# Differential attention in a four-layer kernel: the order of TensorE's products, and where a head's factor is multiplied in

## The reference

```python
L1 = einsum(l2norm(q1), l2norm(k1)) * cos_scale        # b, h, n, m; h = 8 heads, 8 channels each
L2 = einsum(l2norm(q2), l2norm(k2)) * cos_scale
G  = tanh(delta_gain[h] * (L1 - L2))
A1 = softmax(L1 + G)
A2 = softmax(L2 - G)
y  = einsum(A1 - lambda_full * A2, v)
y  = y * rsqrt(mean(y * y) + eps) * subln_weight * 0.5
out = y @ Wo.T + bo
```

## Time and profile before

| | |
|---|---|
| median of 3 runs | 797.56 us (795.8 to 797.76) |
| profiled execution | 796.23 us, span of its instructions 794.0 us |
| busy: TensorE, VectorE, ScalarE, GpSimd | 660.3, 564.8, 485.4, 228.4 us |
| chain of waits that ended last | TensorE 50%, VectorE 30%, ScalarE 11% |
| mean granted TensorE clock | 0.976 of 2.4 GHz |

### The profile page before, as it was taken

The page is one execution under the profiler, slowest core; times in us unless marked ns, Lnnn a source line. Parts: engine busy times, 40 slices in busy tenths (PEclk is TensorE's granted clock), DMA queues, the critical chain, the costliest instruction groups (busy, mean ns, idle before and its releaser), DMA issues.

```text
span 794.0 us, 9725 instructions
## 1 busy us (share of the span) xinstructions
PE 660.3 (83%) x3476; PEld 282.5 (36%) x3514; DVE 564.8 (71%) x1087; ACT 485.4 (61%) x468; POOL 228.4 (29%) x359
## 2 busy tenths in 40 slices
PE   4999899999999478887878788778787787979796
PEld 2576545454544112222221122122222111456364
DVE  5656321407161688888999889999988999768756
ACT  1344323233334359999999999889899989422311
POOL 3601100101014475312434513743933002011001
PEclk9999999999999679999999999999999999999998
DMA  8000200000000110011100111010110013300250
GB/s 296 1 1 1 82 1 0 1 0 1 0 1 0 27 27 14 14 28 28 27 14 19 23 27 28 15 25 15 28 27 14 14 27 107 107 1 14 62 165 27
DMA packets 16752, 26.00 MB, mean 33 GB/s; under 512 B 2496, under 2 KB 7360, under 8 KB 16320
## 3 DMA queue, kind: packets, MB, share of 16 engines
q1 hardware_dynamic: 16704, 25.38, 11.6%
HBM read 15.87 MB, written 1.11 MB: 21 GB/s over the span
## 4 chain that ended last, share of the span: by engine, by line
PE 50%; DVE 30%; ACT 11%; issue 7%; DMA 1%; POOL 0%; SPq 0%; POOLq 0%; ACTq 0%; DVEq 0%
DVE hid L1115 10%; DVE hid L1112 9%; PE ps L512 7%; PE ps L522 7%; ACT probs L821 7%; PE ps L600 6%; PE ps L593 5%; PE ps L612 4%; PE ps L499 3%; ACT w_hh L851 3%; PE ps L621 3%; PE ps L532 2%; PE ps L419 2%; PE ps L450 2%; PE ps L545 2%
## 5 line engine op out<-in xcount | busy, mean ns | idle before, releaser
L851 ACT ACTIVATE w_hh<-hid 128x2048 f32<-128x2048 f32 x128 | 243.8, 1905 | 12.0 <-DVE hid L1115 12.0
L593 PE MATMUL ps<-q_s,k_s 128*128 128x512 bf16 (+1 forms) x474 | 163.4, 394 | 32.4 <-DVE hid L1112 22.2
L1112 DVE TENSOR_TENSOR hid<-ps,probs 128x1024 f32<-128x1024 f32 x128 | 156.3, 1221 | 37.2 <-ACT probs L821 35.9
L821 ACT ACTIVATE probs<-ps,gain 128x1024 f32<-128x1024 f32 x128 | 142.2, 1111 | 40.2 <-PE ps L593 37.0
L1115 DVE SCALAR_TENSOR_TENSOR hid<-ps,probs 128x1024 f32<-128x1024 f32 x128 | 155.4, 1214 | 0.0
L600 PE MATMUL ps<-w_hh,v_h 128*32 128x512 f32 x1024 | 139.4, 617 | 5.4 <-issue 4.4
L593 PE MATMUL ps<-q_w,k_w 64*128 64x512 bf16 x256 | 97.8, 396 | 54.6 <-DVE hid L1115 53.0
L593 PEld LDWEIGHTS ps<-q_s,k_s 128*128 128x128 bf16 (+1 forms) x512 | 42.0, 96 | 148.0 <-DVE hid L1112 60.4
L1449 POOL TENSOR_SCALAR rs<-mv 128x4 f32<-128x4 f32 x32 | 7.4, 231 | 256.5 <-DVE mv L930 256.4
L1023 DVE SCALAR_TENSOR_TENSOR hid<-ps,s_b,rot 128x512 f32<-128x512 f32 x16 | 11.9, 750 | 87.1 <-ACT rot L794 87.1
L877 ACT ACTIVATE u_q<-ps 128x512 f32<-128x512 f32 x32 | 19.1, 598 | 67.8 <-PE ps L612 67.7
(11 more groups left out here) (249 smaller groups left out, 923.3 us busy)
## 6 DMA issues: line engine op xcount, KB each, us to landing
k_w<-k_s SPq DMA_DIRECT2D x32, 128.0 KB, 2.3
q_w<-q_s SPq DMA_DIRECT2D x32, 128.0 KB, 2.3
w_hh<-w_rows SPq DMA_DIRECT2D x4, 1024.0 KB, 10.6
w_hh<-in_b_h SPq DMA_DIRECT2D x2, 1024.0 KB, 8.6
hid<-w_rows SPq DMA_DIRECT2D x2, 1024.0 KB, 6.2
part<-w_rows SPq DMA_DIRECT2D x8, 256.0 KB, 7.3
x_res<-in_x SPq DMA_DIRECT2D x4, 256.0 KB, 6.1
tab<-in_rope SPq DMA_DIRECT2D x1, 1024.0 KB, 7.0
```

The lines of the kernel that those rows point to most:

```text
L593: last = mm(ps[:, base + half, :], k_op[rows, u, keys], q_op[rows, u, half * CHUNK:(half + 1) * CHUNK], start=True, stop=True)
L821: A(gg[:, mt % 2, :], banks[:, 0:2 * CHUNK], ACT.Tanh, scale=gain[:, u:u + 1]).then_inc(S["g"], 1)
L851: A(ee[:, mt % 2, :], zz[:, mt % 2, :], ACT.Exp).then_inc(S["e"], 1)
L1112: v.tensor_tensor(zz[:, mt % 2, 0:SEQ], banks[:, 2 * CHUNK:4 * CHUNK], gg[:, mt % 2, :], ALU.add).then_inc(S["z1"], 1)
```

## The change

The scale of the logits is multiplied by the head's gain before it goes into the queries, so that TensorE's products are gain times L1 and gain times L2, and tanh needs no scale. The two sums multiply the products by the inverse of the gain and by its negative, read through a pointer; the first becomes a scalar_tensor_tensor. The gain is kept between 1e-20 and 1e20 in magnitude. The gain copies on GpSimd and their semaphore go. On TensorE a step's order becomes: difference product (s+2), turn, first component (s+2), values (s), second component (s+2).

```diff
@@ c_table
+            gain = sm[:, SM_GAIN:SM_GAIN + HEADS]
+            me.step(v.scalar_tensor_tensor(tiny[:, 24:32], gain, -1.0, gain, ALU.mult, ALU.max))
+            me.mark(v.tensor_scalar(tiny[:, 24:32], tiny[:, 24:32], GAIN_LOW, GAIN_HIGH, ALU.max, ALU.min))
+            me.step(v.tensor_scalar(tiny[:, 32:40], gain, 0.0, None, ALU.is_ge))
+            me.step(v.tensor_scalar(tiny[:, 32:40], tiny[:, 32:40], 2.0, -1.0, ALU.mult, ALU.add))
+            me.step(v.tensor_tensor(tiny[:, 24:32], tiny[:, 24:32], tiny[:, 32:40], ALU.mult))
+            me.mark(v.tensor_tensor(tiny[:, 8:16], tiny[:, 8:16], tiny[:, 24:32], ALU.mult))
+            me.step(v.reciprocal(gain_inv[:, 0], tiny[:, 24:32]))
+            me.mark(v.tensor_scalar(gain_inv[:, 1], gain_inv[:, 0], -1.0, None, ALU.mult))
@@ TensorE
-            c_scores(0, 0, 0)
-            c_scores(1, 0, 1)
+            for mt in range(2):
+                c_diff(mt, 0, mt)
+                c_first(mt, 0, mt)
+                c_second(mt, 0, mt)
             for n in range(NH):
                 for mt in range(BT):
                     s = n * BT + mt
-                    ...
-                    c_scores(s + 2, u, mt + 2)
-                    ...
-                    c_values(s, u, mt)
-                    use = turning(n, mt)
-                    if use:
-                        c_turning(use)
+                    later = s + 2 < NH * BT
+                    n2, mt2 = divmod(s + 2, BT)
+                    if later:
+                        if mt2 == 0:
+                            pe.wait_ge(S["turn_read"], turns_done(("q", n2)))
+                            pe.wait_ge(S["crossed"], 64 * (n2 + 1))
+                        c_diff(s + 2, n2 % 2, mt2)
+                    use = turning(n, mt)
+                    if use:
+                        c_turning(use)
+                    if later:
+                        c_first(s + 2, n2 % 2, mt2)
+                    ...
+                    c_values(s, n % 2, mt)
+                    if later:
+                        c_second(s + 2, n2 % 2, mt2)
@@ ScalarE
-                A(gg[:, mt % 2, :], banks[:, 0:2 * CHUNK], ACT.Tanh, scale=gain[:, u:u + 1]).then_inc(S["g"], 1)
+                A(gg[:, mt % 2, :], banks[:, 0:2 * CHUNK], ACT.Tanh).then_inc(S["g"], 1)
...
-            act.wait_ge(S["gcp"], 1)
...
-                        act.wait_ge(S["gcp"], n + 2)
@@ VectorE
-                v.tensor_tensor(zz[:, mt % 2, 0:SEQ], banks[:, 2 * CHUNK:4 * CHUNK], gg[:, mt % 2, :],
-                                ALU.add).then_inc(S["z1"], 1)
+                v.scalar_tensor_tensor(zz[:, mt % 2, 0:SEQ], banks[:, 2 * CHUNK:4 * CHUNK], gain_inv[:, 0, h:h + 1],
+                                       gg[:, mt % 2, :], ALU.mult, ALU.add).then_inc(S["z1"], 1)
                 dve.wait_ge(S["l2"], s + 1)
-                v.scalar_tensor_tensor(zz[:, mt % 2, SEQ:2 * SEQ], banks[:, 4 * CHUNK:6 * CHUNK], -1.0,
+                v.scalar_tensor_tensor(zz[:, mt % 2, SEQ:2 * SEQ], banks[:, 4 * CHUNK:6 * CHUNK],
+                                       gain_inv[:, 1, h:h + 1],
                                        gg[:, mt % 2, :], ALU.mult, ALU.subtract).then_inc(S["z2"], 1)
@@ GpSimd
-                if n >= 2:
-                    pool.wait_ge(S["g"], BT * (n - 1))
-                g.tensor_scalar(gain[:, u:u + 1], gains[:, n:n + 1], 1.0, None, ALU.mult).then_inc(S["gcp"], 1)
...
-            pool.wait_ge(ld["cw"], 64)
-            for b in range(BATCH):
-                me.step(g.tensor_scalar(gains[:, b * HEADS:(b + 1) * HEADS], sm[:, SM_GAIN:SM_GAIN + HEADS],
-                                        1.0, None, ALU.mult))
```

More of the change, by code:

```diff
@@ L52 @@
 SM_W = 51
+GAIN_LOW, GAIN_HIGH = 1e-20, 1e20
 NORMS = [("a_in", c) for c in range(4)] + [("a_out", 0), ("b_in", 0), ("a_out", 1), ("a_out", 2), ("a_out", 3),
@@ L206, in sandwich @@
         v_h = sb("v_h", [P, 2, BT, VW])
-        gain = sb("gain", [P, 2])
+        gain_inv = sb("gain_inv", [P, 2, HEADS])
         gg = probs
@@ L242, in sandwich @@
         y_2 = [y[:], rot[:, 0].rearrange("p (a b) -> p a b", a=CT)]
-        gains = sb("gains", [P, BATCH * HEADS])
         ps = ctx.enter_context(nc.psum_tensor("ps", [P, 8, CHUNK], F32))
@@ L257, in sandwich @@
             small_c fact_c
-            uq uk vh gcp turned turn_read crossed dd l1 l2 g z1 z2 e av accout
+            uq uk vh turned turn_read crossed dd l1 l2 g z1 z2 e av accout
             ro to_a ms_o yc ytp yt wo wo_read xn_d tp_d xt_d rt_d z_d tanh_d dist_d ex_d
@@ L582, in router, with c_product, c_diff, c_first @@
                 return last
-            def c_scores(s, u, mt):
+            every, low, high = slice(0, P), slice(0, P // 2), slice(P // 2, P)
+            def c_product(s, u, mt, base, halves):
                 keys = slice(mt * P, (mt + 1) * P)
[L586 to L595, removed]
+                for half, (rows, k_op, q_op) in enumerate(halves):
+                    last = mm(ps[:, base + half, :], k_op[rows, u, keys],
+                              q_op[rows, u, half * CHUNK:(half + 1) * CHUNK], start=True, stop=True)
+                return last
+            def c_diff(s, u, mt):
+                pe.wait_ge(S["g"], s)
+                c_product(s, u, mt, 0, ((every, k_s, q_s), (every, k_s, q_s))).then_inc(S["dd"], 1)
+            def c_first(s, u, mt):
+                pe.wait_ge(S["z1"], s)
+                c_product(s, u, mt, 2, ((low, k_s, q_s), (high, k_w, q_w))).then_inc(S["l1"], 1)
+            def c_second(s, u, mt):
+                pe.wait_ge(S["z2"], s)
+                c_product(s, u, mt, 4, ((low, k_w, q_w), (high, k_s, q_s))).then_inc(S["l2"], 1)
             def c_values(s, u, mt):
@@ L659, in _ @@
             pe.wait_ge(S["crossed"], 64)
-            c_scores(0, 0, 0)
-            c_scores(1, 0, 1)
+            for mt in range(2):
+                c_diff(mt, 0, mt)
+                c_first(mt, 0, mt)
+                c_second(mt, 0, mt)
             for n in range(NH):
-                u = n % 2
                 for mt in range(BT):
                     s = n * BT + mt
-                    if mt < BT - 2:
-                        c_scores(s + 2, u, mt + 2)
[L668 to L672, removed]
+                    later = s + 2 < NH * BT
[10 more added lines that the diff above has]
+                        c_first(s + 2, n2 % 2, mt2)
                     elif mt == BT - 1:
@@ L1106, in _, with z_step @@
             b_y(CHUNKS - 1)
-            def z_step(s, mt):
+            def z_step(s, h, mt):
                 dve.wait_ge(S["g"], s + 1)
                 dve.wait_ge(S["l1"], s + 1)
-                v.tensor_tensor(zz[:, mt % 2, 0:SEQ], banks[:, 2 * CHUNK:4 * CHUNK], gg[:, mt % 2, :],
-                                ALU.add).then_inc(S["z1"], 1)
+                v.scalar_tensor_tensor(zz[:, mt % 2, 0:SEQ], banks[:, 2 * CHUNK:4 * CHUNK], gain_inv[:, 0, h:h + 1],
+                                       gg[:, mt % 2, :], ALU.mult, ALU.add).then_inc(S["z1"], 1)
                 dve.wait_ge(S["l2"], s + 1)
-                v.scalar_tensor_tensor(zz[:, mt % 2, SEQ:2 * SEQ], banks[:, 4 * CHUNK:6 * CHUNK], -1.0,
+                v.scalar_tensor_tensor(zz[:, mt % 2, SEQ:2 * SEQ], banks[:, 4 * CHUNK:6 * CHUNK],
+                                       gain_inv[:, 1, h:h + 1],
                                        gg[:, mt % 2, :], ALU.mult, ALU.subtract).then_inc(S["z2"], 1)
@@ L1278, in _ @@
                     at = (n, mt)
-                    z_step(n * BT + mt, mt)
+                    z_step(n * BT + mt, n % HEADS, mt)
                     use = turning(*divmod(n * BT + mt - 2, BT)) if n * BT + mt >= 2 else None
```

## The result

The changed kernel takes 806.5 us (median of 4 runs, 805.39 to 807.27) against 797.66 (795.8 to 798.01): ratio 1.0114, interval 1.0099 to 1.013. The forecast was 789.5 and faster; the time lies 5.5 us above the range of 778 to 801. The profiled execution takes 807.27 us, its span is 805.5.

A forecast was written before the change was run, and what follows sets the result against it. No engine is full in the attention loop; steps lose time to TensorE's order. Heads 0, 1-3, 4-9, 10-12, 13-15: -1.3, -7.0, -7.5, +9.9, -1.4, sum -7.4 (rounded), putting the median at 790.1, taken as 789.5; range 778 to 801 us.

The forecast's parts named there:

- A new wait: Heads 10 to 12: twelve turns one step after another turn wait for VectorE's copy and delay sums, 13.6 us together.
- The sum: Attention loop, added up by groups of heads from ScalarE's and VectorE's step times, lags and waits: -7.4 us.
- The prediction's walk: Step without a turn: exponential ends 1.9 us after tanh, values 2.9, second product 3.3, next difference product about 3.9.
- Order on TensorE: Loop steps: values run during the second sum, so tanh's wait behind TensorE, 0.57 us in the rows shown, goes.
- Tanh without a pointer: ScalarE's tanh in each loop step: 0.09 us less, making the step 2.70 us instead of 2.79.
- The rival with the saving hidden: Tanh's 0.09 us is hidden on some 50 ScalarE-bound steps: 794 us; chance 0.14, shared with TensorE's order giving less.
- Two sums with a factor: VectorE's two sums per step: the pointer adds 0.06 us each, 15.4 us of VectorE over 256 sums.
- The factor is not free: Answers a rival on VectorE's sums: factor costs nothing back to back, up to 15.4 us less there, 779 us; chance 0.15.
- it doesn't go by column: Answers a rival on VectorE's sums: factor costs by column, 0.12 us a sum, 803 us; chance 0.11.
- Setup: Before the first normalised chunk of queries: eight small VectorE instructions, 1.6 us, covered by 16 us, so cost 0.
- The clock rival: Heads 10 to 12: the twelve new waits lower TensorE's clock, about 0.8 us more each, 798.5 us; chance 0.10.
- Heads 1 to 3 above 23.5 each, sums above 1.3, the waits absent: Signs in the profile after, any of which would show the prediction wrong: head times, sum durations, neighbouring turns' waits (us).

The follow-up runs named there:

- e5: Changed kernel with neighbouring turns put behind the second product and the accumulator's copy between the two sums of tile 1: 782.7 us, 0.9818 of the kernel before.
- e3: Changed kernel with only the twelve turns that follow a turn one step earlier put behind the second product: 788.8 us, 0.989 of the kernel before.
- e4: Changed kernel with only the accumulator's copy moved between the two sums of tile 1: 804.81 us, 1.0081 of the kernel before.
- e13: Changed kernel with the difference product ahead of each neighbouring turn done five times: 803.32 us, 1.0082 of the kernel before.
- e1: Kernel before with only the new order on TensorE, old tanh and sums kept: 801.7 us, 1.0055 of the kernel before.
- e6: e5 with the sums, tanh and unscaled queries of the kernel before: 777.63 us, 0.9764 of the kernel before.
- e8: Changed kernel with a pointer to a one as tanh's scale: 810.35 us, 1.0161 of the kernel before.
- e7: Changed kernel with the old forms of the two sums, leaving out the division by the gain: 794.49 us, 0.9969 of the kernel before.

## Why the prediction was wrong

**The step that failed is "A new wait", twice: it priced the waits of the neighbouring turns too low, and it names no other wait, though there was one.** A third part, 6 us, lies in "The sum", in how far ScalarE and VectorE make up for each other; that part is argued below and not shown. The forecast of the loop was off by 18 us (-7.4 against +10.6). That divides as follows.

*Heads 10 to 12, 8.5 us, most of it the neighbouring turns.* The mechanism was right, in its place, its steps and its kind. The size was 13.6 us. Against e5, in which no sum of these heads waits for TensorE, they took 22.1 more (95.46 less 73.33): 18.6 go with the turns (e3), 5.0 more than priced, and 3.5 with the copy behind that (e5); in the other order the copy alone gave 0.8 (e4), so the two are not cleanly apart. VectorE's groups of that stretch in the kernel after show of what:

```profile
L1132 DVE SCALAR_TENSOR_TENSOR hid<-ps,gain_inv,probs 128x1024 f32<-128x1024 f32 x25 | 32.0, 1278 | 16.5 <-PE ps L598 15.3 <-ACT probs L843 1.2
L1135 DVE SCALAR_TENSOR_TENSOR hid<-ps,gain_inv,probs 128x1024 f32<-128x1024 f32 x24 | 30.7, 1280 | 4.3 <-PE ps L598 4.3
```

First sums waited 15.3 us for TensorE, priced 12.4; second sums 4.3, priced 1.2; and VectorE is busy 2.1 longer than in e5 (74.63 less 72.51): priced nothing. Seventeen sums stand behind a wait for TensorE there and none in e5; a sum behind a pause has no overlap with the instruction before it, and at 0.08 each that is 1.4 us, an estimate. At the upper clock a wait for k or q was 1.11 (priced 0.95: from the turn to the first product 0.55 instead of 0.46, from there to the sum 0.50 instead of 0.45), for another transpose 1.15 (1.1), for a wo product 1.65 (1.5). Of the 4.3 us ahead of second sums 4.0 fall at the five places where the clock was low, and nearly all of it is gone in e13.

*The accumulator's copy, 3.4 us outside heads 10 to 12* (after less e5 in the other four stretches), and part of the 22.1 within them. The prediction asked what TensorE waits for of the turns that the diff moves ahead of a product, and not of the values, which it moves ahead of the second product in the same way. The prediction's walk has the values wait for the exponential alone.

*Lag between engines, 6 us.* Even e5, without either wait, has a loop of 393.0 us, where the prediction's own sum without the new waits, cut at the last sum, gives 386.9 (408.77 - 7.4 - 13.6 - 0.9). Heads 1 to 3 are 1.4 of it (67.95 against 66.5), heads 4 to 9 2.5, heads 13 to 15 2.6. VectorE's busy time was forecast well (139.68 measured in heads 4 to 9, 140.5 forecast), but it stands idle 5.3 us there after the change and 3.8 in e5, where the prediction had less than nothing. A step in which ScalarE is the slower one and a step in which VectorE is do not make up for each other as fully as the walk with its lag supposed. No run here takes that apart; it stays argued.

**Point by point, the rest.**
- *Order on TensorE*: right. The difference product no longer stands behind the values; e1 gives heads 1 to 3 back 4.6 us. Without its two new waits, and with the old sums, it is worth 2.4% (e6, which also has the copy between the sums).
- *Tanh without a pointer*: right, 1111 to 1015 ns, and kept back to back: in head 7 tanh starts at 440.93, the exponential at 441.84 and the next tanh at 443.64, a step of 2.71 us where it was 2.79. With the pointer back, e8 loses 3.9 us. The rival with the saving hidden falls. The Trainium skill (ScalarE: Activation LUTs, What ACT_TABLE_LOAD costs) gives about 93 ns for each pointer operand, and the trace agrees with 96.
- *Two sums with a factor*: right, 1.28 us each; 12.0 of the 15.4 us reach the end (after less e7). The factor is not free, and it doesn't go by column.
- *Setup*: the loop starts at 269.62 instead of 269.33, 0.3 us late, near the 0 that was taken. Over all profiles the loop of the kernels with the factor starts between 269.59 and 270.67, of those without between 268.92 and 269.89, so that it may be up to 1 us.
- *The clock rival* (798.5) was true in kind and about half in size: some 4 us by e13, not 9. The argument against it, that TensorE would be busy some 70% of a step, held (71.94 of 95.46 us is 75%) and yet did not exclude a low clock.
- *Heads 1 to 3 above 23.5 each, sums above 1.3, the waits absent*: none came true (22.9, 1.28, and the waits are there). All three marks of a wrong prediction were passed and the prediction was wrong; the marks tested the terms that it had, and not whether the list was whole.

## What to carry to other kernels

An in-order queue shares every wait with all that stands behind it. When an instruction moves ahead of another one, list all the semaphores that it and its neighbours wait for, the once-a-head ones too, and ask for each who now stands behind it: here twelve turns and fifteen accumulator waits turned a gain of 1.8% (e5) into a loss of 1.1%, with the same order and the same factor otherwise. Price a wait by what it does to the next two instructions of the engine that waits, not to the first alone. Work that is moved from one engine to another is worth what each has to spare: 0.1 us off the tanh and 0.12 onto a pair of sums is a loss where VectorE is the fuller one.

## What the runs showed of the hardware

- A per-partition pointer on a VectorE scalar_tensor_tensor out of PSUM cost 58 to 63 ns at 1024 columns, and 60 at 512 against a tensor_tensor of that width: by instruction, not by column. On ScalarE's tanh it cost 96 ns.
- The granted clock fell to its lower level at five places of heads 10 to 12, though TensorE was busy 75% of the stretch on average. Each time TensorE had stood waiting shortly before or stood waiting then, for 1.19 to 2.85 us (2.10 ahead of the turn at 520.89), but other waits of 1.44 us, as at 526.55, were followed by full speed.

These are TensorE's rows of two short stretches of the kernel after, around the first such place and behind it:

```profile
520.00:523.60 3.60, 2.71 (x18) 0.59 0.00 0
523.60:553.00 29.40, 21.51 (x146) 0.99 0.08 19
```

With repeated products ahead of the same turns (e13) the mean of heads 10 to 12 was 0.98.
